# Running the state-space stage of the next sample in small beats beside attention and convolutions (four-block vision kernel, fp32, one core)

## What is computed

```
x = x + L0(gn(x))     state space, L0 below
x = x + L1(gn(x))     attention, 8 heads of 32, 1024 positions
x = x + L2(gn(x))     four dilated depthwise 3x3 convolutions, a 4x4 mix, a 1x1 convolution
x = x + L3(gn(x))     channel norm, the same attention, channel norm, projection

L0: x, z = split(conv1x1(x));  f1 = conv1x1(x);  f2 = conv2s2(f1);  f3 = conv2s2(f2)
    per level: delta = softplus(...);  h = h * exp(delta * A) + delta * B * x;  y = C . h
    forward and backward over 1024, 256 and 64 positions, 128 channels x 16 states
    y = layernorm(y + D x), levels added up;  out = conv1x1(y * silu(z))
```

## Time and profile before

| | |
|---|---|
| three runs, median (lowest to highest) | 5709.15 us (5706.96 to 5725.84) |
| the profiled execution: time, span | 5702.98 us, 5701.3 us |
| PE, DVE, ACT, POOL busy | 74%, 68%, 37%, 39% of the span |
| DMA | 125 MB, mean 22 GB/s |

### The profile page before, as it was taken

How to read it: one execution, slowest core, us unless ns; L and a number is a source line. 1 busy time by engine, 2 the same in 40 slices (tenths; PEclk the granted TensorE clock), 3 DMA queues, 4 the chain that set the end, 5 groups by cost and what they waited for, 6 DMA issues and landing times.

```text
span 5701.3 us, 44537 instructions
## 1 busy us (share of the span) xinstructions
PE 4237.7 (74%) x16298; PEld 1839.3 (32%) x16298; DVE 3892.5 (68%) x4825; ACT 2109.0 (37%) x2575; POOL 2221.3 (39%) x721
## 2 busy tenths in 40 slices
PE   4678866788658886588865878658786587855878
PEld 2233422333224332243322433223332243322433
DVE  7764788647886478764787646876468774686746
ACT  3233442334423344233442435324253242542424
POOL 4541435414454044540445404444045440454404
PEclk7689977899778997699977999769897798976999
DMA  0020100211002100021000220002200012000120
GB/s 34 0 52 16 30 8 4 49 24 22 8 8 45 33 13 8 8 45 36 10 8 8 45 45 1 8 9 44 45 1 8 18 35 45 8 1 18 27 45 8
DMA packets 58845, 125.24 MB, mean 22 GB/s; under 512 B 14713, under 2 KB 16889, under 8 KB 58370
## 3 DMA queue, kind: packets, MB, share of 16 engines
q1 hardware_dynamic: 58626, 122.39, 9.2%
HBM read 12.23 MB, written 8.39 MB: 4 GB/s over the span
## 4 chain that ended last, share of the span: by engine, by line
PE 44%; DVE 34%; issue 9%; ACT 5%; SPq 4%; POOL 2%; DMA 2%; DVEq 0%; ACTq 0%; POOLq 0%
DVE mx L947 10%; PE PS L1288 8%; PE PS L1246 7%; PE PS L1080 6%; PE PS L1336 6%; PE PS L1370 4%; DVE work L839 3%; PE PS L1139 2%; DVE work L841 2%; PE PS L1180 2%; DVE mboth L954 2%; SPq L284 2%; PE PS L1297 2%; DVE small L714 2%; SPq L293 1%
## 5 line engine op out<-in xcount | busy, mean ns | idle before, releaser
L947 DVE TENSOR_REDUCE mx<-PS 128x1 f32<-128x512 f32 x2048 | 1336.3, 686 | 419.5 <-PE PS L1246 415.2
L617 ACT ACTIVATE PT<-PS 128x1024 f32<-128x1024 f32 x1024 | 1007.4, 1022 | 706.5 <-PE PS L1336 679.1
L1246 PE MATMUL PS<-KS,QS 96*128 96x512 f32 x2048 | 894.7, 479 | 194.6 <-DMA KS<-piece 84.6
L423 POOL TENSOR_TENSOR piece<-PT 128x2048 f32<-128x2048 f32 x48 | 219.9, 4581 | 2000.2 <-ACT PT L617 2000.2
L423 POOL TENSOR_TENSOR piece<-piece,PT 128x2048 f32<-128x2048 f32 x192 | 877.4, 4570 | 61.7 <-ACT PT L617 50.4
L399 POOL TENSOR_TENSOR work<-work,Crep 128x1024 f32<-128x1024 f32 x256 | 615.7, 2406 | 434.2 <-DVE work L839 240.9
L1336 PE MATMUL PS<-QS,KS 98*128 98x512 f32 x2048 | 685.2, 427 | 50.3 <-DMA QS<-nm 32.2
L1246 PEld LDWEIGHTS PS<-KS,QS 96*128 96x128 f32 x2048 | 376.7, 197 | 814.9 <-DVE mx L947 575.1
L1288 PE MATMUL PS<-PT,Vt 128*32 128x512 f32 x4096 | 554.1, 613 | 7.6 <-ACT PT L617 7.6
L1180 PE MATMUL PS<-dstk,sel 128*128 128x512 f32 (+1 forms) x640 | 313.1, 564 | 320.6 <-DVE work L841 133.5
L1180 PE MATMUL PS<-ustk,sel 128*128 128x512 f32 (+1 forms) x640 | 329.4, 587 | 285.4 <-DVE work L824 155.0
(11 more groups left out here) (212 smaller groups left out, 5556.3 us busy)
## 6 DMA issues: line engine op xcount, KB each, us to landing
QS<-piece SPq DMA_DIRECT2D x384, 128.0 KB, 2.4
KS<-piece SPq DMA_DIRECT2D x384, 128.0 KB, 2.4
xin<-x SPq DMA_DIRECT2D x8, 1024.0 KB
out<-xr SPq DMA_DIRECT2D x8, 1024.0 KB, 4.0
W<-wpack SPq DMA_DIRECT2D x2, 1024.0 KB
QS<-nm SPq DMA_DIRECT2D x128, 8.0 KB, 1.9
W<-wpack SPq DMA_DIRECT2D x1, 576.0 KB
W<-wpack SPq DMA_DIRECT2D x2, 256.0 KB
```

Source lines behind the costliest of these rows:

```text
L423: pool.tensor_tensor(total, first, PT[:, i % 3, :, :], ALU.add).then_inc(sum_pool.sem, 1)
L617: act.activation(PT[:, i % 3, 2 * pr:2 * pr + 2, :], PS[:, 2 + 2 * pr:4 + 2 * pr, :], ACT.Exp, scale=SCALE).then_inc(p_sb.sem, 1)
L947: dve.tensor_reduce(mx[:, cc, at:at + 1], PS[:, row_slot(n, cc), :], AX.X, ALU.max).then_inc(r_max.sem, 1)
L1246: pe.matmul(PS[:, row_slot(n, cc), :], QS[0:kd, c, h, q * P:q * P + P], KS[0:kd, h, cc * N:cc * N + N], start=True, stop=True).then_inc(r_ ...
```

## The change

1. **Beats.** Every engine's code of attention, convolutions and norms calls `beat(mark)` at the same places (363 per sample); at each call one piece of a generator `state_space(b + 1)` is issued: 15 beats for the front, 62 for each of four chunks (14 of preparation, 48 of 16 steps), 74 for the short levels, 337 in all. The stage of the first sample runs alone, before the loop.
2. **512 columns at a time.** The two long passes are four chunks of 512 columns; the state at a chunk's end goes by `carry` (POOL copies it) into the next chunk's scan. Of the eight PSUM banks the stage has three: `Y` (5), `U` (6) and `D` (7), one each for sums, inputs and step sizes. Preparation, products and norms keep temporaries in these banks or in tiles of 512 columns.
3. **Attention on five banks.** Scores alternate between two banks and ACT takes one head (512 columns) at a time. Row scores have one pair of banks, and DVE reduces 1024 columns at once; `mboth` is gone. 22 row tiles stand before the first phase; the other 42 are placed by `row_plan`, one at every even beat of a key tile, and none in the last phase. Denominators: POOL adds six of eight key tiles in all four phases, 1024 columns at a time; PE adds two. The bias of the output goes from DVE to ACT.
4. **Memory.** The stage has tiles of its own beside attention. Sample, next sample and output use the place of `QS`; the weights of the projections are loaded anew for each attention, and those of the stage's front for each sample. The ones in `KS` are written once.
5. Depthwise filters use 64 x 64 tiles of the array in place of 128 x 64.

The core of the diff:

```diff
-HALF_ROWS = (5, 4, 4, 4, 5, 5, 5, 0)
-PHASE_ROWS = sum(HALF_ROWS) // NC
-POOL_SUMS = (0, 1, 2, 3, 5, 6)
-DVE_SUMS = (0, 1, 2, 3, 4, 5, 6)
+FIRST_ROWS = PHASE_ROWS + 6
+POOL_ADDS = 5
+CHUNKS = [(0, 0), (0, 1), (1, 1), (1, 0)]
+PREP = 14
+CHUNK_BEATS = PREP + 3 * SG
+LOW_BEATS = 74
+FRONT_BEATS = 15
...
+    def __call__(self, mark):
+        self.marks.append(mark)
+        next(self.part, None)
...
-            work = so("work", [P, 12, L])
...
+        BCs = sb("BCs", [P, 2, N])
+        dstk = sb("dstk", [P, 2, N], F32R)
+        ustk = sb("ustk", [P, 2, N], F32R)
+        ring = sb("ring", [P, 8, N])
+        dBx = sb("dBx", [P, 2, N])
+        carry = sb("carry", [P, SG])
...
+        Y, U, D = 5, 6, 7
```

On PE, an expansion of the stage and the row scores of attention:

```diff
+                def expand(k, i, first, spans):
...
+                    else:
+                        pe.wait_ge(*dBx_sb(b, i))
+                        pe.wait_ge(*scanned(b, scans_to(i - 1)))
+                    for bank, stk, done in ((U, ustk, u_ps), (D, dstk, d_ps)):
+                        for at, n, lo, w in spans:
+                            g = scan_group(n)
+                            ins = pe.matmul(PS[:, bank, at:at + w], sel[:, g % 8, :], stk[:, g // 8, lo:lo + w],
+                                            start=True, stop=True)
+                        ins.then_inc(done.sem, 1)
...
+                        s, off = divmod(t - PREP, 3)
+                        if s >= 0 and off == 0:
+                            expand(k, SG * k + s, s == 0, [(0, s, 0, N)])
...
+            def row_scores(b, a, r):
...
+                if r > 0:
+                    pe.wait_ge(*r_max(b, ROWS * a + r))
...
+                for cc in range(NC):
+                    ins = pe.matmul(PS[:, 3 + cc, :], QS[0:96, c, h, q * P:q * P + P], KS[0:96, h, cc * N:cc * N + N],
+                                    start=True, stop=True)
+                ins.then_inc(r_ps.sem, 1)
```

On ACT the decay (beat with off 1) and on DVE product (off 1), scan (off 2) and row maximum:

```diff
+                        if s >= 0 and off == 1:
+                            i, ps = SG * k + s, CHUNKS[k][0]
+                            at = ps * SG + scan_group(s)
+                            act.wait_ge(*d_ps(b, i + 1))
+                            act.activation(PS[:, D, :], PS[:, D, :], ACT.Exp, scale=Aneg[:, at:at + 1]).then_inc(dA_sb.sem, 1)
...
+                        if s >= 0 and off == 1:
+                            inputs(SG * k + s, (1, 0, N))
+                        if s >= 0 and off == 2:
+                            scan_main(k, s)
...
+                    dve.tensor_tensor_scan(slot_of(i)[:, way], PS[:, D, way], dBx[:, i % 2, way], first, ALU.mult,
+                                           ALU.add).then_inc(scanned.sem, 1)
...
+                dve.tensor_reduce(mx[:, ph % 2, at:at + 1], flat(PS[:, 3:5, :]), AX.X, ALU.max).then_inc(r_max.sem, 1)
```

On POOL the product by C with the carry, and a denominator sum:

```diff
+                    pool.wait_ge(*scanned(b, scans_to(i)))
+                    pool.wait_ge(*c_sb(b, k + 1))
+                    if k in (0, 2):
+                        edge = (N - 1, 0)[k // 2]
+                        pool.tensor_copy(carry[:, s:s + 1], slot[:, edge:edge + 1]).then_inc(carried.sem, 1)
+                        pool.wait_ge(*carried(b, SG * (k // 2) + s + 1))
+                    pool.tensor_tensor(slot, slot, BCs[:, 1, :], ALU.mult).then_inc(hC_sb.sem, 1)
...
+                                pool.tensor_tensor(acc[:, two, :], first, PT[:, i % 3, two, :], ALU.add).then_inc(summed.sem, 1)
```

More of the change, by code:

```diff
@@ new lines, in attention @@
+                if a == 0 and b + 1 < B:
+                    act.wait_ge(*z_ps(b + 1, 2))
+                    act.wait_ge(*f3_ps(b + 1, 1))
+                for r in range(FIRST_ROWS):
+                    if r % 2 == 0 and r < 8:
+                        q = r // 2
+                        act.wait_ge(*v_ps(b, 4 * a + q + 1))
+                        act.activation(flat(Vt[:, 2 * q:2 * q + 2, :]), PS[:, (8 + q) % 3, :], ACT.Copy).then_inc(v_sb.sem, 1)
+                    if r == PHASE_ROWS:
+                        neg_max(b, a, 0)
+                    beat(("row", r))
@@ new lines, in attention, with neg_max @@
+                beat("last values")
+                beat("last sums")
+                reciprocals(b, a, PHASES - 1)
+                beat("last reciprocals")
+                add_bias(b, a, PHASES - 1, bq)
+                beat("last bias")
+            def neg_max(b, a, ph):
+                n = PHASES * a + ph
+                act.wait_ge(*mt_ps(b, n + 1))
+                if b + n > 0:
+                    act.wait_ge(*nm_in(b, 32 * n))
+                act.activation(nm[:, 0, :], PS[0:PHASE_ROWS, 3, 0:P], ACT.Copy, scale=-1.0).then_inc(nm_head.sem, 1)
@@ L657, in _ @@
-                group_norm(b, 4, xin)
-                act.wait_ge(*x_new(b, 16))
+                beat.finish()
+            tail(B - 1)
         @block.vector
@@ new lines, in attention, with residual @@
+                beat("last values")
+                beat("last sums")
+                beat("last reciprocals")
+                normalize(b, a, PHASES - 1)
+                beat("last bias")
+            def residual(b, first, banks, src, dst, bias, mark, norm):
+                for n, (m, c) in enumerate(ORDER):
+                    cs = slice(c * N, c * N + N)
+                    dve.wait_ge(*o_ps(b, first + n + 1))
+                    dve.scalar_tensor_tensor(out=dst[:, m, cs], in0=PS[:, banks[n], :], scalar=v(bias, m),
+                                             in1=src[:, m, cs], op0=ALU.add, op1=ALU.add).then_inc(x_new.sem, 1)
+                    if norm and n > 0:
+                        dve.wait_ge(*x_new(b, first + n))
+                        stats(gn, xr, *ORDER[n - 1])
+                    beat((mark, n))
+                if norm:
+                    dve.wait_ge(*x_new(b, first + 4))
+                    stats(gn, xr, *ORDER[3])
@@ L1428, in summed @@
-def summed(a, ph, kt):
-    sums = POOL_SUMS if ph < PHASES - 1 else DVE_SUMS
-    if kt not in sums:
-        return None
-    k = max(1, sums.index(kt))
-    return (0, pool_sums(a, ph, k)) if ph < PHASES - 1 else (1, dve_sums(a, k))
+                beat.finish()
+            tail(B - 1)
+        assert all(m == marks["pe"] for n, m in marks.items() if n != "sp")
 def scan_group(n):
```

2131 lines of the change are left out of this document (1141 added, 990 removed).

## The result

| | before | after |
|---|---|---|
| median of four runs | 5708.06 us | 6279.24 us (6270.93 to 6283.7) |
| ratio | | 1.099, 95% interval 1.097 to 1.102 |
| span of the profiled execution | 5701.3 us | 6269.2 us |

The account below looks back on a forecast made before the run. The prediction took the order of instructions, one beat over single PSUM banks, as the bound. First stage 386, first sample 638, six samples of 658 and last sample 503 sum to 5475, stated as 5480 us; range 5150 to 5870.

Parts of the forecast that it names:

- 1.53 us a beat: Attention phases with row tiles: six beats take 9.2 us; taken as 1.56, 50 us a phase of 32 beats.
- order is the bound: Whole sample: instruction order over single PSUM banks, not busy time, sets the beat; 658 us a sample, chance 0.42.
- the walk: Phases with row tiles: instruction-by-instruction timing of two scan steps and three row tiles, 8.6 us, plus 0.6 for blocks.
- rival 1: PE's clock falls, half the time low in phases and first rows: 1.8 a beat, 420 us more, 5900 us; chance 0.20.
- Rival 2: DVE hardly waits; phases at POOL's pace, 45 us, gaps in norms and head vanish: 610 a sample, 5145 us; chance 0.18.
- Rival 3: POOL decides: late products hold PE at the state sums, 1.7 a beat in the phases, 5676 us; chance 0.14.
- Rival 4: POOL's additions hold DVE's port in five masks and four norms a sample: 147 us more, 5630 us; chance 0.06.
- The first stage: First sample's state-space stage, run alone: loading, front, five preparations, 64 steps of 3.0, short levels, last norms: 386 us.
- The last sample: Final sample, with no stage beside it but single row banks: 184 us per attention, 503 us in all.
- head: Start of a sample: norm and output of the last sample, gating, first norm, plus the front: 51 us.
- jobs: Eight projection jobs per attention, two fp32 matmuls each, 2.3 us a beat: 18 us per attention, 36 for both.
- the stage between: Projection, convolutions and norms between the two attentions: 78 us before, forecast 89 with 23 beats in it.

Follow-up runs that it names:

- the run that held the clock at 1.00: Changed kernel with five extra 512-column matmuls in front of each PE wait for the last scan: 6183 us.
- 2: Changed kernel with decay, product and scan of the long-pass steps issued one beat earlier: 5890 us, 389 less than the changed kernel.
- the better order: Changed kernel with all scan steps a beat earlier, first row tiles on alternating banks, and input expansion not waiting for the last scan: 5599 us.

## Why the prediction was wrong

- **The step that failed** is the price of one beat in the phases with rows: "So 9.2 us, **1.53 us a beat**", taken as 1.56 and a phase of 50 us. They took 61 us, 1.92 a beat. The mechanism "order is the bound" was right, and two things in the sum were too small. At the full clock the two kinds of step shown take 4.90 + 5.42 = 10.3 us for six beats, 1.72 a beat, which makes an estimate of 55 us a phase. And all of it was costed at full clock, while the phases ran at 0.80 to 0.86.
- **In the walk** most of the missing 1.1 us is in the steps as such. The step without a block takes 4.90 us, the walk's second step 4.37: product and scan take 0.88 + 1.28 us there (the scan stands 0.20 behind its own product, and PE waits for its full end), where the walk had 0.60 + 1.12. The walk's 0.6 for value product and state sums was near for the full clock: six beats hold about two such blocks, but only some of them stand between expansion and row scores (in 37 of the 76 steps timed at that clock), and there one costs 0.5 to 0.9 us; in the step shown DVE makes its product meanwhile. At 0.50 it costs 2.4.
- **The clock** is the other half, by estimate 6 of the 11 us of a phase: 61 measured, 55 by the full-clock steps, and 56.3 in the run that held the clock at 1.00. The text had named 0.85 as the point from which rival 1 decides, and gave it 0.20. Its 2.1 us a beat at the lower clock was too low as well: 5.8 + 8.2 us for six beats are 2.3. It put 420 us on the clock; extra matmuls gave 83 and 96, a net that leaves the clock's own price open. With the order mended, the clock rose without any extra work in the two phases named under 2. The Trainium skill (TensorE: Matmul & The Clock Gate, section on psum-queue depth-cycling) says of another kernel that small idle times between groups make the clock alternate. The trace agrees that it alternates: within one phase the stretch from 2178 to 2184 us lies at 0.50 and that from 2190 to 2196 at 1.00.
- **DVE** was to be 70 to 75% busy in the phases with idle time put down to PE: the cause is right, the share is 56 to 59%.
- **Rival 2** (DVE hardly waits) had the sizes right and is refuted by 1237 us of idle time in front of the maxima. It would need the better order and still more: there phases with rows took 46 to 57 us, not 45.
- **Rival 3** (POOL): the cut of its additions left the phases where they were. In the better order it is worth 1.9%.
- **Rival 4** (DVE held at its port): almost none of it. The mask (line 981) takes at most 0.70 us in all its 40 instances, the copy behind it the same. What the forecast had cited from the Trainium skill (SBUF — State Buffer, shared port pair) finds one case in this trace, the norm's product of 1024 columns from SBUF to SBUF (line 905). It takes 0.81 us, and 1.92 in two of 24 instances, both beside POOL's product by C; together 2.2 us. In the version of 5599 us it happens once in each of seven samples.

```profile
1575.20 1.92 DVE L905 TENSOR_SCALAR xg<-xr,small 128x1024 f32<-128x1024 f32 x1
...
1575.30 1.28 POOL L427 TENSOR_TENSOR ring<-ring,BCs 128x512 f32<-128x512 f32 x1
```

- **The first stage** was 57 us off: its first scan came at 80.7 us instead of about 65, the 64 steps took 3.4 us, not 3.0, and the stretches of preparation between the chunks about 20, not 17. The 3.0 were costed at full clock, though the earlier trace rows had shown 0.70 in the scans of before, and the earlier trace rows a price at the lower one. That is the same omission, where the rows were already in hand.
- **The last sample** (50 us too long) has nothing beside it, so this part of the miss does not come from the beats: an attention took 211 us instead of 184. The rows took 51.6 us instead of 48 at a clock of 0.67, the four stretches behind them 144 instead of 121, the first of them 47.7 at 0.86 and the others at 1.00.
- **Right:** head 51 against 49.7, jobs 36 against 38.7, the stage between 89 against 82.6, the durations of DVE and ACT to 2%; POOL's are 4 to 7% longer (1.28 against 1.2, 2.37 against 2.29). Most of the error lies where engines wait for one another in a circle.

Open: the product's place by itself, how the 389 us divide between order and the clock that follows it, and what the low clock costs the changed kernel as a whole.

## What to carry to other kernels

When a second piece of work is dealt out in beats beside the first, let the reader of a single buffer be issued in the same beat as its writer's result or the next, ahead of the host's own work on that engine; one beat of place, without any work saved, was worth 6% here. In a walk through such a circle price each kind of step by itself, give the instruction that releases the next engine its full length, and do the walk at both levels of the granted clock: a block of eight short matmuls cost 0.5 to 0.9 us at one and 2.4 at the other. Price each part alone in its new form first: here that cost 1,739 us before anything was gained. A lower bound by busy time (here 420 us a sample) says nothing about a chain across four engines with single buffers (754); first ask how many beats the scan's end lies ahead of who waits for it.

## What the hardware showed

- TensorE's granted clock was 0.50 from 80 to 130 us in the first stage, with PE busy 23 of 50 us. Five matmuls in its waiting time brought 0.91 and a step of 2.81 in place of 3.37 us, with 135 matmuls against 54 in these 50 us. It was no constant gain: from 300 to 350 us of the same run the clock was 0.76. Beside attention the trick gave 61 us of 6279, 1.0%, and 65 with two matmuls.
- A scan of 512 columns takes 1.22 us from a constant start and 1.28 from a start value in SBUF: 0.06 us for the carry on DVE, and 0.19 on POOL for its copy.
- POOL's work did not slow DVE's operations on PSUM: scans, products and maxima each keep one duration to 3% in the whole run, with POOL busy 65% of a phase or idle. The norm's SBUF-to-SBUF operation took 1.92 us instead of 0.81 beside it.
